# Moving weight DMAs from GpSimd to the sync queue, and four scan units ahead of the FFN, in an SSM and ternary-FFN layer

## The reference, cut to what matters

```python
delta = softplus(x @ Wd.T + bd)
a_pos = softplus(a_log) + 0.0001
def step(state, (x_t, delta_t)):            # state: [batch, 1024, 16]
    state = exp(-dt * a_pos) * state + dt * b_param * x_t
    return state, state.sum(-1)
y = scan(step) @ Wo.T + bo
# FFN, bitlinear(x, w) = act_quant(x) @ weight_quant(w).T
#   weight_quant: scale = 1 / mean|w|, w -> clip(round(w * scale), -1, 1) / scale
#   act_quant:    per row, 127 / max|x|, round
out = bitlinear(silu(bitlinear(x, w_gate)) * bitlinear(x, w_up), w_down)
```

## Time and profile before

| | us |
|---|---|
| two runs of the kernel | 4227.61 and 4237.48, median 4232.55 |
| the profiled execution | 4227.07 |
| its span on the slowest core (core 4) | 4225.5 |
| the other cores' spans | 4206.8 to 4218.1 |
| PE busy | 1295.6 (31%) |
| DVE busy | 1497.5 (35%) |
| ACT busy | 1450.1 (34%) |
| POOL busy | 331.0 (8%) |

### The profile page before, as it was taken

How to read it: one execution, slowest core, us unless ns; L and a number is a source line. 1 busy time by engine, 2 the same in 40 slices (tenths; PEclk the granted TensorE clock), 3 DMA queues, 4 the chain that set the end, 5 groups by cost and what they waited for, 6 DMA issues and landing times.

```text
span 4225.5 us, 25493 instructions; the slowest of 8 cores (4206.8 to 4225.5 us)
## 1 busy us (share of the span) xinstructions
PE 1295.6 (31%) x5181; PEld 532.3 (13%) x5260; DVE 1497.5 (35%) x2016; ACT 1450.1 (34%) x2106; POOL 331.0 (8%) x527
## 2 busy tenths in 40 slices
PE   1122120000110112012462632461632555516553
PEld 0100000000000001000221210221210222103221
DVE  0067846880000001000047893147893132021410
ACT  3544333333542543345322333232333211132201
POOL 0012212220000000000001230000000000000000
PEclk9965555555555555555685665785655786658766
DMA  4000011003324330334320101120101220112111
GB/s 64 0 0 1 0 20 50 30 20 124 100 85 155 104 104 25 129 99 122 111 94 13 41 29 40 53 97 0 45 25 40 70 80 30 40 40 90 60 40 50
DMA packets 121338, 245.36 MB, mean 58 GB/s; under 512 B 6113, under 2 KB 71906, under 8 KB 117090
## 3 DMA queue, kind: packets, MB, share of 16 engines
q1 hardware_dynamic: 99170, 159.57, 11.5%
q0 software_dynamic: 22016, 84.15, 6.9%
HBM read 218.80 MB, written 33.55 MB: 60 GB/s over the span
## 4 chain that ended last, share of the span: by engine, by line
DVE 25%; PE 21%; ACT 21%; DMA 16%; issue 10%; POOL 6%; ACTq 1%; DVEq 1%; POOLq 0%; SPq 0%
DVE s_sig L289 11%; POOL s_state L263 5%; PE pU L846 5%; PE pG L838 5%; PE pD L966 4%; DVE s_sig L296 4%; DMA wu_buf<-wu 3%; DMA wdn_buf<-wdn 3%; DMA wg_buf<-wg 3%; DMA s_td<-tdT 2%; DVE s_ytmp L313 2%; ACT s_h L928 2%; PE ptD L921 2%; PE pW L663 2%; DVE s_qs L870 2%
## 5 line engine op out<-in xcount | busy, mean ns | idle before, releaser
L282 ACT ACTIVATE s_abar<-s_dyq,s_nega 128x512 f32<-128x512 bf16 x512 | 369.4, 722 | 610.3 <-DVE s_sig L289 463.1
L289 DVE TENSOR_TENSOR_SCAN s_sig<-s_abar,s_state,s_lnf 128x512 bf16<-128x512 f32 x384 | 492.8, 1283 | 123.1 <-ACT s_abar L282 73.7
L966 PE MATMUL pD<-s_td,s_h 128*128 128x512 bf16 x1000 | 386.4, 567 | 223.0 <-DMA s_td<-tdT 213.7
L838 PE MATMUL pG<-s_tg,s_dyq 128*128 128x512 bf16 x980 | 380.2, 388 | 115.8 <-DVE s_h L865 115.5
L846 PE MATMUL pU<-s_tu,s_dyq 128*128 128x512 bf16 x1024 | 397.0, 388 | 27.7 <-DMA s_tu<-tuT 21.4
L313 DVE SCALAR_TENSOR_TENSOR s_ytmp<-s_sig,s_bprm,s_ytmp 128x512 bf16<-128x512 bf16 x448 | 336.4, 751 | 48.9 <-DVE s_sig L289 2.3
L263 POOL TENSOR_TENSOR s_state<-s_sig,s_onesp 128x1 bf16<-128x1 bf16 x384 | 247.3, 644 | 1052.9 <-DVE s_sig L289 502.0
L865 DVE TENSOR_TENSOR s_h<-s_gtmp,pU 128x512 bf16<-128x512 bf16 x128 | 87.9, 687 | 661.7 <-ACT s_gtmp L858 661.7
L858 ACT ACTIVATE s_gtmp<-pG,s_r1g 128x512 bf16<-128x512 f32 x128 | 88.0, 687 | 419.2 <-PE pU L846 249.5
L966 PEld LDWEIGHTS pD<-s_td,s_h 128*128 128x128 bf16 x1024 | 135.5, 136 | 473.0 <-issue 459.3
L663 PE MATMUL pW<-s_w,s_dyq 128*128 128x512 bf16 x251 | 92.3, 544 | 322.9 <-DVE s_x L683 197.2
(11 more groups left out here) (165 smaller groups left out, 1803.1 us busy)
## 6 DMA issues: line engine op xcount, KB each, us to landing
s_tg<-tgT SPq DMA_DIRECT2D x64, 512.0 KB, 3.4
s_tu<-tuT SPq DMA_DIRECT2D x64, 512.0 KB, 4.8
s_td<-tdT SPq DMA_DIRECT2D x64, 512.0 KB, 3.6
wg_buf<-wg SPq DMA_DIRECT2D x16, 1024.0 KB, 5.1
wg_buf<-wg POOLq DMA_DIRECT2D x16, 1024.0 KB, 6.8
wu_buf<-wu SPq DMA_DIRECT2D x16, 1024.0 KB, 5.3
wu_buf<-wu POOLq DMA_DIRECT2D x16, 1024.0 KB, 7.0
wdn_buf<-wdn SPq DMA_DIRECT2D x16, 1024.0 KB, 5.1
```

What stands on the lines that cost most here:

```text
L282: lambda h, d=dc, n_=n, p=pa: h.activation(out=s_abar[:, p, :], in_=delta_view[:, d, t0:t0 + QT], func=AF.Exp, scale=s_nega[:, d, n_:n_ + 1]),
L289: lambda h, d=dc, c_=col, p=pa, s=ps: h.tensor_tensor_scan(s_sig[:, s, :], s_abar[:, p, :], lnT_view[:, d, t0:t0 + QT], s_state[:, c_:c_ + 1],
L838: h.matmul(pGs[c_][:], q1T_view[:, k, t_ * 128:(t_ + 1) * 128], s_tg[:, wp, k4_, :], start=(k == 0), stop=(k == KC - 1)),
L966: lambda h, c_=c, k=kc, p=par, s_=sub, f=hf: h.matmul(pDs[c_][:, f * 512:(f + 1) * 512], q2T_view[:, c_, k, :], s_td[:, p, s_, f * 512:(f ...
```

## The change

Three DMA sites lose their choice of queue and are issued by SP: the slice loads of both passes and the stage store. Waits and semaphores are the same.

Between `emit_C_q(0)` and the barrier, four units of quarter 2 are emitted. The other twelve go into a list `bpend`; `pop_B(k)` emits the next k. Every group takes one behind oc 3, one behind oc 6 and up to six behind the transposes: group 0 eight units (quarter 2's last four, quarter 3's first four), group 1 the remaining four, groups 2 and 3 none. Before, groups 0 and 1 took eight each.

```diff
@@ abs pass
-                sch.dma("sync" if par % 2 == 0 else "gpsimd", f"wbuf{par}",
+                sch.dma("sync", f"wbuf{par}",
@@ sign pass, slice load
-                                sch.dma("sync" if par4 % 2 == 0 else "gpsimd",
-                                        f"wbuf{par4}",
+                                sch.dma("sync", f"wbuf{par4}",
@@ sign pass, stage store
-                    t_st2 = sch.dma("gpsimd", "stage_st",
+                    t_st2 = sch.dma("sync", "stage_st",
@@ behind emit_C_q(0) and the last units of quarter 1
         t_y_q = {1: ST("vector")}
+        for dc in range(4):
+            emit_B_dc(2, dc)
+        bpend = [(2, dc) for dc in range(4, KC)] + [(3, dc) for dc in range(KC)]
+
+        def pop_B(k):
+            while k > 0 and bpend:
+                qq, dc = bpend.pop(0)
+                emit_B_dc(qq, dc)
+                if dc == KC - 1:
+                    flush_save(force=True)
+                    t_y_q[qq] = ST("vector")
+                k -= 1
         sch.barrier()
@@ gate/up loop
-                        if g < 2 and oc in (3, 6):
-                            emit_B_dc(g + 2, oc // 3 - 1)
+                        if oc in (3, 6):
+                            pop_B(1)
@@ behind the transposes
-                if g < 2:
-                    for dc in range(2, KC):
-                        emit_B_dc(g + 2, dc)
-                    flush_save(force=True)
-                    t_y_q[g + 2] = ST("vector")
+                pop_B(6)
```

## The result

The changed kernel takes 4240.25 us (median of 26 runs, 4230.91 to 4251.04) against 4231.84 (median of 25, 4217.02 to 4238.61). The ratio is 1.0023, interval 1.0016 to 1.0031: 8 to 10 us slower, where 53 to 57 were forecast. The time lies at the lower end of the stated range, the direction is right, the size is not.

The account below looks back on a forecast made before the run. No engine was taken to bound the kernel, a row of stages with different limits. Against 4227.1 us, -112.5 + 78.5 + 145 - 54 = +57 gave 4284, taken as 4285; range 4240 to 4325.

Parts of the forecast that it names:

- Abs passes: Abs passes of wg, wu and wdn: loads on SP run ahead and stream at 3.3 us per further MB, -112.5 us together.
- Sign passes: Sign passes of wg, wu and wdn: each load waits behind the stage store on SP, +78.5 us, bounds about +30 and +145.
- The 2 MB store: wdn's sign pass: at three borders the load right behind this store lands after 16.6 us, +4 a border, +12 us.
- The row pair: Sign passes of wg and wu: every one takes 17.9 us with store and load on SP, +33 and +33.5 us.
- Four units ahead of the barrier: Between wdn and the barrier: four scan units lie bare, 4 x 35.6 us plus some 2.5 us, +145 us.
- Group 1: FFN group 1: with two scan units behind its transposes instead of six, the eviction follows PE at once, -54 us.
- The dear queue: Sign passes: a load behind a store moves nothing until the store lands, 20 us a row pair, 4350 us; chance 0.12.
- The case without streaming: Abs passes: each MB takes 5.1 us, so the gain is 80 instead of 112, 4317 us; chance 0.09.
- The cheap queue: Sign passes: the load overlaps the store wholly, 16.3 us a row pair, -48, so 4237 us; chance 0.06.
- The hidden units: Ahead of the barrier: scans run under wdn's loads and evictions, the +145 fall away, 4140 us; chance 0.03.

Follow-up runs that it names:

- part A alone: All slice loads and the stage store issued by SP, scan units as before, against the kernel before: 4147.28 us, ratio 0.9815.
- part B alone: Four scan units moved ahead of the barrier, all queues as before, against the kernel before: 4314.76 us, ratio 1.0197.
- the store alone: Only the stage store moved to SP, slice loads alternating between queues as before, against the kernel before: 4188.74 us, ratio 0.9915.
- the loads-only kernel: All slice loads issued by SP, stage store left on POOL (GpSimd), against the kernel before: 3981.78 us, ratio 0.9418.

## Why the forecast was wrong, step by step

**Abs passes: right in sum.** Forecast -112.5, measured -109.8 in the changed kernel and -114.9 in part A alone. Two errors partly cancel: wu gained 39.0 us instead of 36.5, wdn 34.9 instead of 40. The estimate of 3.3 us for each further MB came from the difference between a 1 MB and a 512 KB load. In wu ACT's passes of slices 4 and 15 (timeline of ACT, changed kernel) lie eleven intervals of 3.16 us (the mean) apart:

```profile
1276.57 1.91 ACT L484 ACTIVATE wu_tern<-wu_buf 128x2048 bf16<-128x2048 f32 x1 [2.13 <-DMA wu_buf<-wu]
...
1311.29 1.91 ACT L484 ACTIVATE wu_tern<-wu_buf 128x2048 bf16<-128x2048 f32 x1 [0.77 <-DMA wu_buf<-wu]
```

So the queue streams between that estimate and an estimated 2.9 us a MB from the 358 GB/s of the Trainium skill (DMA: Bandwidth & Descriptors, Specifications).

**Sign passes: the step that failed.** The mechanism was right: the load stands behind the store and ACT waits 7.3 us for it in every row pair. The sum was +78.5 and the chip shows +36.9 (part A alone +32.6). Two terms were mis-sized, in the same direction.

- The 2 MB store. I carried the 16.6 us of the earlier trace rows over to SP unchanged. On SP the load behind it lands after 11.5 to 12.4 us (12.6 to 13.7 in part A alone), in the mean 4.7 us sooner than I had put it: 14 of the 20 us by which wdn's sign pass, -8.3 instead of +12, was too dear. Another 3 lie in its first row pair, ahead of any store, which I had put at nothing; SP's quicker answer (below) gives some 2. The row was one of POOL's queue, with a load of SP's beside it. The change moves that very transfer to another queue and takes the other queue's loads away, so it was a row of another case; no store from SP of this kind existed in the trace, and I should have put a bound on it from both sides as for the rest.
- The row pair. Forecast 17.9 us, measured (1222.44 - 981.29) / 14 = 17.2. The way from the store's issue to ACT's start was right, 7.1 forecast, 7.21 here. The other leg, from ACT's start to the next store, was kept at 10.83 and is 10.07. Over half of the difference is the queue's answer: in the row pair shown SP issues the store 0.08 us after the last eviction's end (1084.24 + 0.38 to 1084.70). POOL took 0.54 us, as this row of the kernel before, the eviction ahead of the store at 1083.83, shows:

```profile
1082.91 0.38 ACT L537 ACTIVATE wg_stage<-wg_ptb 128x256 bf16<-128x256 bf16 x1
```

  The remaining 0.3 us stay open. 30 row pairs x 0.7 = 21 us.

These two are the 41 us by which the sign passes were too dear. A term that is repeated 30 times turns 0.7 us into half of this miss.

**Four units ahead of the barrier: right.** Forecast +145, measured +140.6; 4 x 35.7 = 143 us (the row from 1984 to 2127), less the quicker last store. The 2.5 us for a table load and the start of the pipe were not paid: the first exponential starts at 1984.40, 0.2 us after the last store landed, and the timeline of ACT has no table load ahead of it.

**Group 1: right in mechanism.** Forecast -54, measured -62.9 in group 1 and -57.7 for the whole FFN, since group 2 became 5.8 us longer, which no run explains (group 2 took 501 to 512 us in the profiles). The experiments bracket the limit of the cover between four and six units; that it is near four follows from 142 against 152 us.

**The rivals.** The dear queue (the load starts when the store has landed) is excluded by the row pair: the load at 1085.15 lands after 6.5 us, where the store's 3.5 and a load's 5.1 one after the other would make it 8.2. The case without streaming is excluded by the 3.16 us. The cheap queue's *time*, 4237, is nearly what came out, but not by its mechanism: loads behind the store land after 6.3 and not after 5.1 us; half came from the leg with the queue's answer, half from wdn. The hidden units are excluded by part B alone, +83.

**The range.** It began at 4240, and the median is 4240.25, so that the time lies in it at all is luck; the size of the change is a fifth of the forecast. I had also taken 2% as what a measurement can tell from no change; the interval of the result is 0.15% wide. What made it so is that the forecast is a small difference of large terms: -110, +37, +141, -58. An error of half of one term is most of the sum. The bound of the sign passes was from 30 to 145; the measured 37 lies within, at an end to which I gave 0.06, because it was drawn for one cause only.

## What to carry to other kernels

Before moving a DMA to another queue, write down that queue's program around it: a transfer that waited for a computed result stopped every prefetch behind it. Here one line, the store on the loads' queue, is worth 168 us (0.9815 against 0.9418). In this kernel it pays to have loads on one queue and stores that wait on another. And ask of each scan unit, or other filler, which wait ends last where it stands: behind a 152 us down projection four units of 36 us cost nothing, ahead of a barrier each costs all of it, and the fifth and sixth behind the projection together cost 63 of their 71 us.

## What the runs showed of the hardware

- A 2 MB stage store with no load beside it landed after 8.7 to 9.0 us when SP issued it (the changed kernel, part A, the store alone) and after 10.7 to 10.8 when POOL did (before, the loads-only kernel). With loads queued behind it on SP it took 9.0 to 10.0 us in the same three runs; from POOL, with a load of SP's queue beside it, 13.9 to 15.3 in those two. For 512 KB the medians are 3.2 to 3.5 against 3.8 to 3.9 us. The trace counts 4112 packets for the last 2 MB store of the changed kernel, from SP, and 528 for that of the kernel before, from POOL.
- A 1 MB load alone landed in 5.0 to 5.2 us from either queue (1825.70 on SP and the earlier trace rows on POOL, kernel before; 1760.24 on SP, changed kernel).
- SP issued a stage store 0.07 to 0.08 us after the eviction that it waited for had ended (six row pairs of wg, changed kernel), POOL 0.53 to 0.71 us after (seven row pairs of wg, kernel before).
- With loads queued on SP in a ring of four, one MB followed another at 3.16 us in the mean. From 1276 to 1312 us, in this stretch, the DMA share is 0.75 to 1.00 on all eight cores.
